# A semaphore of its own for each expert weight load in an attention and mixture-of-experts layer

## The reference, cut to what matters

```python
x = _layernorm(x + attn(x))      # window attention and linear attention, 16 heads
x = _layernorm(x + ffn(x))
# ffn: 8 experts, all computed for all tokens, the best two weighted
logits = xt @ gate_w.T + gate_b
top_v, top_i = jax.lax.top_k(logits, 2)
h0 = jnp.einsum('td,ehd->eth', xt, w0) + b0[:, None, :]
h1 = jnp.einsum('td,ehd->eth', xt, w1) + b1[:, None, :]
act = h0 * jax.nn.silu(h1)
out_all = jnp.einsum('eth,edh->etd', act, w2) + b2[:, None, :]
```

## Time and profile before

| | us |
|---|---|
| median of 4 runs | 10,741.05 |
| lowest and highest | 10,735.03 and 10,833.94 |
| the profiled execution | 10,757.63 |
| its span on the slowest core (core 1) | 10,756.1 |
| spans of the eight cores | 10,717.8 to 10,756.1 |
| PE busy | 7,083.9 |

### The profile page before, as it was taken

The page is one execution under the profiler, slowest core; times in us unless marked ns, Lnnn a source line. Parts: engine busy times, 40 slices in busy tenths (PEclk is TensorE's granted clock), DMA queues, the critical chain, the costliest instruction groups (busy, mean ns, idle before and its releaser), DMA issues.

```text
span 10756.1 us, 104659 instructions; the slowest of 8 cores (10717.8 to 10756.1 us)
## 1 busy us (share of the span) xinstructions
PE 7083.9 (66%) x37091; PEld 3432.7 (32%) x37091; DVE 1830.6 (17%) x4145; ACT 2676.0 (25%) x3877; POOL 869.6 (8%) x1530
## 2 busy tenths in 40 slices
PE   3443887887334388788734438878873443887886
PEld 1221333343122134344312224434431222443442
DVE  2222111111222211111122221111112222111111
ACT  1221222223222122222322212222231221222223
POOL 1121000000112100000011200000001120000000
PEclk8565998998656599899865659989986555998998
DMA  3003335232300223423130032442413003243241
GB/s 51 8 1 48 49 59 86 49 59 38 63 8 1 48 49 63 81 49 64 33 63 8 1 48 49 68 77 49 68 28 63 5 1 48 49 78 67 49 80 33
DMA packets 243920, 493.80 MB, mean 46 GB/s; under 512 B 14032, under 2 KB 14032, under 8 KB 243408
## 3 DMA queue, kind: packets, MB, share of 16 engines
q0 software_dynamic: 225424, 453.02, 25.8%
q1 hardware_dynamic: 17984, 34.09, 1.0%
HBM read 923.32 MB, written 16.78 MB: 87 GB/s over the span
## 4 chain that ended last, share of the span: by engine, by line
PE 65%; DMA 10%; ACT 7%; POOL 6%; issue 5%; DVE 4%; another core or an unknown queue 3%; DVEq 0%; ACTq 0%; POOLq 0%; SPq 0%
PE pb L90 36%; PE pbA L90 15%; PE pbB L90 10%; DMA arena<-w2t 8%; ACT arena L90 6%; POOL arena L90 6%; PE pT L90 4%; DVE arena L90 2%; DMA arena<-x 1%; ACT t L90 1%; DVE smal L90 1%; DMA arena<-gb 0%; DVE t L90 0%; DMA out<-t 0%
## 5 line engine op out<-in xcount | busy, mean ns | idle before, releaser
L90 PE MATMUL pb<-arena 128*128 128x512 bf16 (+2 forms) x19328 | 3949.1, 368 | 1094.9 <-DMA arena<-w2t 835.9
L90 PEld LDWEIGHTS pb<-arena 128*128 128x128 bf16 (+1 forms) x19328 | 1861.1, 103 | 3159.1 <-issue 1265.0
L90 ACT ACTIVATE arena<-pb,arena 128x512 bf16<-128x512 f32 x2048 | 1407.5, 687 | 3051.7 <-PE pb L90 2954.3
L90 PE MATMUL pbB<-arena 128*128 128x512 bf16 (+1 forms) x5504 | 1088.8, 343 | 1104.2 <-POOL arena L90 973.4
L90 PE MATMUL pbA<-arena 128*128 128x512 bf16 x6656 | 1544.3, 393 | 126.8 <-DMA arena<-wout 79.2
L90 DVE TENSOR_TENSOR arena<-arena 128x512 bf16<-128x512 bf16 (+13 forms) x1536 | 654.1, 426 | 4031.3 <-ACT arena L90 2920.5
L90 PEld LDWEIGHTS pbB<-arena 128*128 128x128 bf16 x5504 | 527.8, 104 | 1655.8 <-issue 1172.6
L90 PEld LDWEIGHTS pbA<-arena 128*128 128x128 bf16 x6656 | 668.1, 101 | 972.5 <-issue 242.9
L90 PE MATMUL pT<-idbf,arena 128*128 128x128 bf16 (+1 forms) x3072 | 416.0, 304 | 804.8 <-DVE arena L90 560.5
L90 ACT ACTIVATE arena<-pT 128x512 bf16<-128x512 bf16 (+1 forms) x576 | 368.7, 640 | 1268.9 <-PE pT L90 1244.8
L90 DVE TENSOR_TENSOR t<-t,arena 128x1024 f32<-128x1024 f32 x256 | 313.6, 1225 | 1593.6 <-ACT arena L90 1593.6
(11 more groups left out here) (84 smaller groups left out, 1902.0 us busy)
## 6 DMA issues: line engine op xcount, KB each, us to landing
arena<-w2t POOLq DMA_DIRECT2D x32, 4352.0 KB, 29.3
arena<-w0t POOLq DMA_DIRECT2D x64, 2048.0 KB, 17.4
arena<-w1t POOLq DMA_DIRECT2D x64, 2048.0 KB, 26.0
arena<-x SPq DMA_DIRECT2D x32, 512.0 KB, 4.0
arena<-wout POOLq DMA_DIRECT2D x4, 4096.0 KB, 65.8
out<-t SPq DMA_DIRECT2D x4, 4096.0 KB, 13.9
arena<-wq POOLq DMA_DIRECT2D x4, 2048.0 KB, 18.1
arena<-wk POOLq DMA_DIRECT2D x4, 2048.0 KB, 31.6
```

The source lines that it names most:

```text
L90: r = getattr(e, meth)(*args, **kw)
```

## The change

Each weight load and bias load of an expert counts on a semaphore of its own. The values of the tokens are still replaced by the count planned so far, but of that semaphore alone. One wait is added for a debug output, which this build does not make (`dbg` is False, so the token is None).

```diff
-DMA_SEMS = {"dx", "dw", "do"}
+DMA_SEMS = {"dx", "dw", "do", "dw00", "dw01", "dw10", "dw11", "dw2", "dbb0", "dbb1"}
...
             t00 = OP("gpsimd", "dma_start", out=pw03[:, :, 0:1024],
                      in_=self.w0t_h[e, :, 0:1024].rearrange("(s p) w -> p s w", p=128),
-                     after=[a00], inc=("dw", 16))
+                     after=[a00], inc=("dw00", 16))
             t10 = OP("gpsimd", "dma_start", out=pw13[:, :, 0:1024],
...
-                     after=[a10], inc=("dw", 16))
+                     after=[a10], inc=("dw10", 16))
...
-                     after=[a01], inc=("dw", 16))
+                     after=[a01], inc=("dw01", 16))
...
-                     after=[a11], inc=("dw", 16))
+                     after=[a11], inc=("dw11", 16))
             t2 = OP("gpsimd", "dma_start", out=pw23,
                     in_=self.w2t_h[e, :, :].rearrange("(s p) w -> p s w", p=128),
-                    after=[a2], inc=("dw", 16))
+                    after=[a2], inc=("dw2", 16))
             tb0 = OP("sync", "dma_start", out=self.b0col[:, :],
-                     in_=self.b0r_h[e, :, :], after=[ab], inc=("dx", 16))
+                     in_=self.b0r_h[e, :, :], after=[ab], inc=("dbb0", 16))
             tb1 = OP("sync", "dma_start", out=self.b1col[:, :],
-                     in_=self.b1r_h[e, :, :], after=[ab], inc=("dx", 16))
+                     in_=self.b1r_h[e, :, :], after=[ab], inc=("dbb1", 16))
...
-                             after=[tsc2, acc_tok[j]], inc="v")
+                             after=[tsc2, acc_tok[j], self.dbg_t1_tok], inc="v")
```

More of the change, by code:

```diff
@@ L243, in __init__ @@
         self.pl = Plan()
-        for sn in ["t", "v", "s", "g", "dx", "dw", "do"] + ["b_" + e for e in ENGS]:
+        for sn in (["t", "v", "s", "g", "dx", "dw", "do",
+                    "dw00", "dw01", "dw10", "dw11", "dw2", "dbb0", "dbb1"]
+                   + ["b_" + e for e in ENGS]):
             self.pl.new_sem(sn, E(nc.semaphore("sem_" + sn)))
@@ L962, in phase_B @@
                     in_=self.G_s[:, 8 * j:8 * (j + 1)], after=[g_tok], inc=("dx", 16)))
+        self.dbg_t1_tok = None
         if self.dbg:
-            self.dbg_toks.append(OP(
+            self.dbg_t1_tok = OP(
                 "sync", "dma_start",
@@ L967, in phase_B @@
                 in_=self.t1.rearrange("p (c w) -> p c w", c=8),
-                after=[self.ln_tok[7], trt], inc=("dx", 16)))
+                after=[self.ln_tok[7], trt], inc=("dx", 16))
+            self.dbg_toks.append(self.dbg_t1_tok)
         self.load_act(self.SET_SILU)
```

## The result

The changed kernel takes 9,642.6 us (median of 7 executions), the kernel before 10,798.3 us (median of 10 executions beside it); the ratio of the changed kernel to the kernel before is 0.896, with a 95% interval of 0.892 to 0.900. In some executions of every kernel here, before as well as after, the cores of one die, now and then of both, read a lower granted clock (0.81 in dense stretches on core 2 in the trace of experiment 3) and take up to 12% longer, so all ratios, and all times but these two medians, are of executions without it, or, where there was none, of the cores of a die without it. The profiled execution took 9,641.0 us, with spans of 9,622.1 to 9,639.2 us on the eight cores. The forecast was 9,625 us in a range of 9,590 to 9,790.

What follows compares the result with a forecast made beforehand. TensorE was taken to bound the kernel, idling for w2t loads it did not yet need. Core 0: 10,743.7 - 1,047.9 + 4 - 60 = 9,640, plus 1.5 to execution, minus 16.6 to median: 9,625 us, range 9,590 to 9,790.

Steps and rivals of the forecast that it cites:

- the plan's rule for DMA tokens: All five expert-phase loads count on semaphore dw; every wait is for its whole count so far, hence for w2t too.
- Term 1: TensorE's waits on w2t ahead of experts' first matmuls and the gate's go: 1,072.7 us on core 1.
- Term 2: At the gate, the last eviction of the transposes is late next: 1 us idle four times, 4 us stay.
- Term 3: Slow restart of an expert's first 256 matmuls after a pause goes: 2.14 us, 28 times, 60 us.
- Term 4: Every expert load hides behind matmuls: 0 us; w2t takes 35 to 38.5 us, needed after 55.4, cover 17 at least.
- Late halves: TensorE catching up with a late half load of w0 or w1: up to 5 us at 28 boundaries, 140 us.
- the worst case of 52.5 us: Longest time of a half-expert load, behind three others; counted from 1,211.41 it ends at 1,264, before 1,270.
- The sum: Core spans less pauses, plus 4, minus 60: cores 0, 1, 7 at 9,640, 9,627, 9,624 us; median forecast 9,625.
- Rival A: Clock falls in unbroken expert stretches; with a quarter of matmul work at 1.2 GHz 10,997 us, 2.4% slower; chance 0.04.
- Rival B: Wait moves to the first w2 matmul: 23 us each, 704 us come back, 10,330 us; chance 0.04.
- Rival C: Another load shares a semaphore, so the old waits stay: 10,741 us; chance 0.01.

Runs made afterwards that it cites:

- experiment 3: Changed kernel, but each expert after the first waits for its w2 load before its first matmul; 10,512.0 and 10,524.2 us, ratio to the kernel before 0.978.
- Experiments 1 to 3: The first: kernel before with an own semaphore for the gate's weights alone, cores 0 to 3 spanned 10,607 to 10,622 us; then experiment 2 and experiment 3.
- Experiment 4: Kernel before, with 130 extra matmuls ahead of each of the 28 boundary waits; 10,698.6 and 10,712.1 us, ratio to the kernel before 0.9958.
- experiment 2: Kernel before, with an own semaphore for w2 alone, the other expert loads still sharing one; profiled execution of its second run 9,765.3 us.
- experiment 5: Changed kernel, but each expert after the first waits for its w2 load at hidden slice 8, not the w2 stage; cores spanned 9,663 to 9,692 us.
- run 9: The text given has no run of this name, neither in the kept part nor in the dropped parts.

## Why the prediction was right

**The cause.** The trace had the wait on w2t at two places that don't read w2, and the plan's rule for DMA tokens explained it. Experiments 1 to 3 undo and do its parts one by one, and each puts the pauses where that rule puts them.

**Term 1, the pauses.** Forecast 1,072.7 us on core 1, all of it; no row of such a wait is left.

**Term 2, the gate.** Forecast 1 us of idle time four times. Measured: 1.01 us at the first, and the wait of pb on VectorE rose from 43.9 us in 32 times to 47.9 us in 36.

**Term 3, the clock.** Forecast 60 us. The 28 stages behind a pause took 57.50 us on average on core 1, 58 us in all above 55.42, and all of them take 55.4 now. PE's busy time fell by only 52.3 us on this core, since the pbA matmuls of the attention phases took 11.3 us more (651.6 instead of 640.3); over the eight cores it fell by 52.3 to 72.6. Experiment 4 shows that the slow restart is the clock.

**Term 4, each load hides.** Right in its conclusion, wrong in its size: 29 to 32 us for w2t beside matmuls instead of 35 to 38.5, which only widened the cover. Late halves, for which the range had 140 us, cost nothing: the changed kernel has no wait on w0t or w1t, and even where all halves are due at the boundary they cost 1.3 us in all on core 6 (experiment 2). One of the term's steps doesn't hold as written: the worst case of 52.5 us was counted from 1,211.41, the issue of w01, but w11 was issued at 1,230.07 and would have landed by it at 1,282.6, behind the 1,270 at which it was needed. It was not put to the test, since w11 now goes out at once.

**The sum.** For core 0 the forecast was a span of 9,640 us, the measured one is 9,636.6; for the profiled execution 9,641.5 us, and 9,641.0 were measured. That this agrees within a microsecond is in part luck. Core 0 is not the slowest; core 1 is, at 9,639.2 us where its sum gave 9,627, and core 7 took 9,637.9 where its sum gave 9,624. On core 1 most of these 12 us are the 11.3 us of the attention phases' matmuls, which the sum had no term for. The step that was off in the forecast of the median is the last one: I took 16.6 us off, because the profiled execution of the kernel before had been that much above its median. Those 16.6 us were probably core 1's longer loads, since it waited 24.8 us more on w2t than core 0, and the change had just removed them from the sum; no other execution of that run was traced, so this is argued and not shown. Taking them off again made the forecast 17 us too low.

**Rival A, the clock.** Not seen in the profiled execution. From 1,010 to 2,380 us core 1 works without rest, with a granted clock of 0.99 over the whole stretch, the slow start of the first expert included:

```profile
1010.10:2380.00 1369.90, 1355.52 (x6272) 613.98 (x6272) 189.71 (x338) 435.15 (x595) 33.45 (x35) 0.99 0.45 70
```

and late in it, from 2,100 to 2,250, all eight cores read 1.00 (the first of eight rows):

```profile
2100.00:2250.00 150.00, 150.00 (x696) 67.99 (x695) 20.65 (x37) 48.73 (x68) 4.78 (x5) 1.00 0.57 86
```

The rule of the Trainium skill ("TensorE: Matmul & The Clock Gate", section "Seeing it yourself") takes a die to 13/16 of the clock once three of its cores run dense matmuls. 13/16 is the 0.81 of the first section; but eight cores in dense matmuls at 1.00, late in eight unbroken experts, don't agree with it as a rule for every execution.

**Rival B, a wait at the w2 stage,** has no row on any of the eight cores, and experiment 5 shows some 25 us of cover to spare. **Rival C** is excluded by the missing waits.

## What to carry to other kernels

Where a wait is made for the full count of a semaphore, as in this plan, it is as late as the last transfer that counts on it, not as the one it needs; so look, for every long wait on a DMA, whether the instruction behind it reads that DMA's tensor. If it doesn't, follow the freed engine to the next wait before pricing the gain: the gate freed alone was worth the 29 us of its own work per quarter, and its pause of 59 only once the expert behind it was free too. And before an excess of the profiled execution is taken off on the way to the median, look whether it sits in the wait that the change removes, for then it is gone already.

## What the runs showed that I had not expected

How short a rest already costs PE its clock. In experiment 4, 2.3 to 4.5 us of idle time made the next 256 matmuls 1.3 to 2.9 us longer in 14 cases of 15, hardly less than a pause of 30 us does (2.1 us on average), while 2.2 us or less cost nothing in 31 cases. The line between the two is not sharp: on cores 0 to 3 of experiment 5, rests of 2.00, 2.07 and 2.19 us each made the next stretch 1.7 us longer, and one of 2.02 us did not. A pause that is filled to nine tenths can therefore keep much of the restart's price. And the 4,352 KB load took hardly longer with PE busy (medians of 29.2 to 31.6 us on the eight cores) than with PE idle (27.9 to 29.3).
